# Attention over growing key blocks, masks added by TensorE, and weight splits moved between stages of a fused attention and expert kernel

## The reference

```python
q_sem, q_geo = 16 heads of 32; k_sem, k_geo, v = 4 groups;  q_geo, k_geo roped
remote = Tq - LW                      # 1024 - 128 = 896; nblk = 14 blocks of 64
pool = mean over each block of 64 for the first 896 keys, then the last 128 keys as they are
k_pos = concat(arange(14) * 64 + 63, arange(896, 1024))      # 142 keys
scores = (q_sem @ k_sem2 + q_geo @ k_geo2) / sqrt(32) * exp(logit_scale)
scores = where(k_pos <= pos, scores, -1e9)
out = softmax(scores) @ v2, then @ Wo
# expert branch: router softmax over 16 experts, top 4, weights normalised
out = sum over the 4 of weight * (silu(x @ gate) * (x @ up)) @ down
```

## Time and profile before

| What | Value |
|---|---|
| Median of 3 runs | 415.14 us |
| The profiled execution's own time | 414.26 us |
| Its span, first to last instruction | 412.5 us |
| TensorE busy | 367.9 us, 89% |
| VectorE busy | 263.2 us, 64% |
| ScalarE busy | 185.9 us, 45% |
| GpSimd busy | 233.3 us, 57% |
| Mean granted TensorE clock | 0.959 |

### The profile page before, as it was taken

How to read it: one execution, slowest core, us unless ns; L and a number is a source line. 1 busy time by engine, 2 the same in 40 slices (tenths; PEclk the granted TensorE clock), 3 DMA queues, 4 the chain that set the end, 5 groups by cost and what they waited for, 6 DMA issues and landing times.

```text
span 412.5 us, 8607 instructions
## 1 busy us (share of the span) xinstructions
PE 367.9 (89%) x2263; PEld 309.1 (75%) x2264; DVE 263.2 (64%) x837; ACT 185.9 (45%) x537; POOL 233.3 (57%) x205
## 2 busy tenths in 40 slices
PE   0599995968998999799899999999999999999991
PEld 0483474756885677577678899999999999999881
DVE  4889244897924799999857755555555555555540
ACT  1541236543521265225537655555555555555550
POOL 3501556566555435994605666566666666666664
PEclk9999997897999999999779999999999999999996
DMA  7991222212114963068545666676667667667544
GB/s 246 357 316 46 78 78 78 78 64 92 52 66 143 319 208 110 21 195 222 152 141 101 104 107 116 103 110 110 111 106 112 114 106 112 112 106 112 78 52 51
DMA packets 49016, 51.41 MB, mean 125 GB/s; under 512 B 5472, under 2 KB 46048, under 8 KB 48992
## 3 DMA queue, kind: packets, MB, share of 16 engines
q0 software_dynamic: 14640, 19.34, 28.3%
q1 hardware_dynamic: 34352, 31.78, 27.2%
HBM read 29.67 MB, written 21.43 MB: 124 GB/s over the span
## 4 chain that ended last, share of the span: by engine, by line
PE 71%; DVE 14%; issue 7%; ACT 3%; DMA 2%; SPq 1%; POOLq 1%; another core or an unknown queue 0%; DVEq 0%; ACTq 0%
PE bank L1292 59%; PE bank L1654 4%; PE bank L1678 4%; DMA x_all<-in_L_attn_x 1%; ACT lex L760 1%; DVE q L1073 1%; DVE q L1070 1%; ACT x_all L692 1%; PE bank L1445 1%; PE bank L1416 1%; DMA out_rows<-y,idx 1%; DVE l L1097 1%; DVE pr L1213 1%; DVE xr L1241 1%; DVE pr L1233 1%
## 5 line engine op out<-in xcount | busy, mean ns | idle before, releaser
L670 POOL DMA_INDIRECT out_rows<-y,idx x79 | 122.9, 1556 | 81.8 <-ACT y L854 63.2
L648 POOL DMA_INDIRECT xn_by_expert<-x_all,slot_i x64 | 64.9, 1014 | 20.4 <-issue 15.7
L1272 DVE SCALAR_TENSOR_TENSOR act<-bank,xg,sg 128x224 f32<-128x224 f32 x79 | 35.6, 450 | 51.5 <-ACT sg L841 50.7
L1292 PE MATMUL bank<-wgu_hi,xh 128*128 x158 | 65.2, 413 | 0.5 <-issue 0.2
L1292 PE MATMUL bank<-wgu_lo,xh 128*128 x158 | 58.5, 370 | 0.0
L1292 PE MATMUL bank<-wgu_hi,xl 128*128 x158 | 57.9, 366 | 0.0
L841 ACT ACTIVATE sg<-bank 128x224 f32<-128x224 f32 x79 | 28.3, 358 | 60.6 <-PE bank L1292 59.7
L1264 DVE TENSOR_TENSOR xl<-bank,xh 128x256 fp32r<-128x256 f32 x79 | 33.5, 424 | 29.4 <-ACT xh L834 29.1
L1292 PE MATMUL bank<-wdn_hi,ah 112*128 x158 | 51.3, 324 | 0.5 <-issue 0.4
L1292 PE MATMUL bank<-wdn_hi,al 112*128 x158 | 44.4, 281 | 0.0
L1292 PE MATMUL bank<-wdn_lo,ah 112*128 x158 | 44.2, 280 | 0.0
(11 more groups left out here) (238 smaller groups left out, 766.1 us busy)
## 6 DMA issues: line engine op xcount, KB each, us to landing
xg<-xn_by_expert SPq DMA_DIRECT2D x79, 129.0 KB, 2.5
wgu<-in_L_ffn_gate_proj SPq DMA_DIRECT2D x16, 224.0 KB, 5.4
wgu<-in_L_ffn_up_proj SPq DMA_DIRECT2D x16, 224.0 KB, 5.8
wdn<-in_L_ffn_down_proj SPq DMA_DIRECT2D x16, 224.0 KB, 6.2
x_all<-in_L_attn_x SPq DMA_DIRECT2D x8, 256.0 KB, 4.8
xr<-in_L_attn_x SPq DMA_DIRECT2D x14, 128.0 KB, 4.6
out_rows<-xr SPq DMA_DIRECT2D x14, 128.0 KB
out_rows<-y,idx POOLq DMA_INDIRECT x79
```

The source lines that it names most:

```text
L648: gp.indirect_dma_start(xs_d, bass.IndirectOffsetOnAxis(slot_i[:, z, r:r + 1], 0), x_all[:, z, :], None).then_inc(xs_in[q], DMA)
L670: gp.indirect_dma_start(out_rows, bass.IndirectOffsetOnAxis(idx[r % RING][:, 0:1], 0), ysb[r % 4][:, :], None, compute_op=ALU.add).then_in ...
L1272: nc.vector.scalar_tensor_tensor(av[t.par][:, :], bank[2 + t.par][:, I:2 * I], xg[t.slot][:, D + 1:D + 2], sg[t.par][:, :], ALU.mult, ALU. ...
L1292: return nc.tensor.matmul(o, lhsT, rhs, start=start, stop=stop)
```

## The change

Six things change together.

1. **Remote scores**: the columns are laid out block by block, with the 16 heads inside a block, so that tile t needs only the first 32(t+1) of 224 columns. Matmuls, exponentials and VectorE's operations take only those. For tiles 1 to 6 the mask is a bf16 matmul of the identity with `hide_b` over the last 32 columns, and VectorE reads maximum and subtraction directly from PSUM; the masking operation and the copy of `even` are gone. Tile 0 keeps the masking operation on 32 columns, and gets the even part through a matmul with the constant `even`. The probabilities need one transpose and one matmul for tiles 0 to 3 (plus the even part in tile 0), two after that.
2. **Local scores**: the mask is the first matmul into each bank (bf16, identity with `hide_lb`). VectorE takes four negated maxima directly from PSUM, one for each head, and ScalarE reads PSUM for the exponentials. The banks come free only when the exponentials are done, in two pairs of heads.
3. **Tables and folding**: `weights(2)`, `weights(3)`, the first part of the task plan and `bd_s` move ahead of the local queries on VectorE, the rest of the plan (`bound_tasks`) right behind them.
4. **Values**: `build_values` needs one multiplication per group, `sum_columns` goes. The folding with Wo is one matmul of 58 rows x 512 per group in units 3 to 6. Its rows go to DRAM and come back as `vw` in the new order: 12 writes and 3 reads on SyncE's queue.
5. **Splits**: ScalarE makes the high parts of experts 0 to 3 in remote pairs 0 and 1, 4 to 9 in pairs 3 to 5, 10 to 12 at the head of the expert loop, and 13 to 15 at steps 5, 6, 7. VectorE makes the low parts of 0 to 5 at the end of pairs 0 to 5 and 13 to 15 at steps 6, 7, 8. GpSimd makes 6 to 12, and starts when VectorE has made its six.
6. **SyncE**: the residual rows of pair 6 are loaded early, experts 10 to 12 in one group, 13 to 15 behind the first eight task loads.

```diff
-LATE = ((4, 5), (6, 7), (8, 9), (10, 11), (12,), (13, 14, 15))
+LATE = ((4, 5), (6, 7), (8, 9), (10, 11, 12), (13,), (14,), (15,))
-ON_DVE = 4
+ON_DVE = 6
-        SPLITS = ((), (4, 5), (6, 7), (8, 9), (), (10, 11), (12,))
+        SPLITS = ((0, 1), (2, 3), (), (4, 5), (6, 7), (8, 9), ())
+        HEAD = (10, 11, 12)
@@ ScalarE: local exponentials; head and steps of the loop
-                    last = nc.scalar.activation(lex[q][:, h, :], l2[q][:, h, :], ACT.Exp, bias=lneg[q][:, h:h + 1], accum_out=lsum[q][:, h:h + 1])
-                last.then_inc(l_ex, 1)
+                    nc.scalar.activation(lex[q][:, h, :], bank[L_BANKS[h]][:, 0:NKEY], ACT.Exp, bias=lneg[q][:, h:h + 1], accum_out=lsum[q][:, h:h + 1]).then_inc(l_ex, 1)
...
+                    for k in HEAD:
+                        split_late(k)
...
-                if j.counts is None and j.r in (1, 3, 5):
-                    split_late(IN_LOOP + j.r // 2)
+                if j.counts is None and j.r in (5, 6, 7):
+                    split_late(IN_LOOP + j.r - 5)
@@ SyncE: the folded values through DRAM
+            for g in range(HKV):
+                sp.wait_ge(fold_kept, g + 1)
+                for m in range(2):
+                    sp.dma_start(vw_rows[:, :, 2 * g + m, :], folded[g % 2][0:FOLD - NB, m, :]).then_inc(folded_out[g % 2], DMA)
...
+            sp.dma_start(vw[:, :, 0, :], by_batch[0:P, :, :]).then_inc(vw_in, DMA)
@@ VectorE: local scores
-                for h in range(G):
-                    last = nc.vector.tensor_tensor(l2[q][:, h, :], bank[L_BANKS[h]][:, 0:NKEY], hide_l, ALU.add)
-                last.then_inc(l_read, 1)
-                dve.wait_ge(l_read, n + 1)
-                link(nc.vector.tensor_reduce(lmax[q][:, :], l2[q][:, :, :], axis=AX.X, op=ALU.max))
-                nc.vector.tensor_scalar(lneg[q][:, :], lmax[q][:, :], -1.0, None, ALU.mult).then_inc(l_max, 1)
+                for h in range(G):
+                    last = nc.vector.tensor_reduce(lneg[q][:, h:h + 1], bank[L_BANKS[h]][:, 0:NKEY], axis=AX.X, op=ALU.max, negate=True)
+                last.then_inc(l_max, 1)
@@ VectorE: remote pairs
+                scores = bank[6 + u]
+                if t.first:
...
+                link(nc.vector.tensor_reduce(smax[u][:, :], by_head(scores, t), axis=AX.X, op=ALU.max))
...
+                nc.vector.tensor_tensor(by_key(pr[u], t), by_key(scores, t), over_heads(smax[u][:, :], t), ALU.subtract).then_inc(c_d[u], 1)
...
+                if t.number < ON_DVE:
+                    split_low(t.number)
@@ TensorE: local scores
-                    pe.wait_ge(l_read, n)
...
+                for two in ((0, 1), (2, 3)):
+
+                    if n:
+                        pe.wait_ge(l_ex, G * (n - 1) + two[1] + 1)
+                    for h in two:
+                        mm(bank[L_BANKS[h]][:, 0:NKEY], ident_b[:, :], hide_lb[:, :], True, False)
@@ TensorE: folding, remote scores
+                mm(bank[4][0:FOLD, :], vb[:, g, :], wo_s[:, 2 * g:2 * g + 2, :].rearrange("p m d -> p (m d)"), True, True).then_inc(fold_done, 1)
...
+                    mm(bank[6 + u][:, 0:t.cols], xT[t.number][:, u, c, :], asem[:, u, c, 0:t.cols], c == 0, False)
+                if not t.first:
+                    mm(bank[6 + u][:, t.cols - 2 * H:t.cols], ident_b[:, :], hide_b[:, :, :].rearrange("p k h -> p (k h)"), False, False)
```

337 lines of the change are left out of this document (174 added, 163 removed).

## The result

The changed kernel takes 419.43 us, the median of 20 executions (414.79 to 427.65), where the kernel before took 414.89 beside it (20 executions, 412.82 to 416.87). The ratio is 1.0083, 95% interval 1.0056 to 1.0110. Forecast was 398.5, a ratio near 0.96.

A forecast was written before the change was run, and what follows sets the result against it. Bounds: a TensorE-VectorE-ScalarE ring in the local units, VectorE in the remote pairs, TensorE in the expert loop. From 414.26 us profiled, -7.5 - 14.2 + 0 + 4.5 + 1 = -16.2 gave 398.1; stated 398.5, range 389.5 to 408.5.

The forecast's parts named there:

- Local units: Local attention stage: last exponentials end at 107.5, `l_attend` starts at 110.5 instead of 118.04 us, -7.5 us.
- The ring: Local units' cycle through TensorE, VectorE and ScalarE: 4.0 us a turn, 4.8 with value folding, 6.6 with queries too.
- Rival (d): Local units 2 to 7 and output products: TensorE idles each turn, clock stays at 1.2 GHz, 423 us; chance 0.08.
- Tables ahead and the values' way through DRAM: Before and during local units: tables hidden by VectorE's waits, DRAM trip ending near 113 us; 0 us each.
- Output products: Products between local units and remote pairs: stay at 13.0 us.
- Remote pairs: Remote attention: VectorE's pairs 0 to 5 take 53.5 us, first tokens turned at 185.6 instead of 207.35; -14.2 us.
- A page against it: VectorE's PSUM reads: a skill page's rule adds 65 ns to each of 60 operations, making 402.4 us.
- Head: Start of expert loop: ScalarE's three splits cost about 2.0 us, no lower clock gives -2.0; sum 0.
- GpSimd's gate: Expert loop: GpSimd's seven splits start after VectorE's sixth, so ScalarE's result 4 waits for the scatter; +4.5 us.
- T: End of VectorE's remote pair 5, forecast at 182.0 us; GpSimd's first result scatter lands at T + 29.9.
- Splits 13 to 15: Loop's head: these experts' splits in three consecutive steps instead of every second add VectorE work; +1 us.

The follow-up runs named there:

- e13_fill6: e10_early_fill5 plus a sixth fill, 6 throwaway TensorE products ahead of unit 7's scores: 404.09 us, ratio 0.9726.
- e11_before_fill: The kernel before plus 43 throwaway TensorE products at waits in local units 0, 1 and 4: 409.46 us, ratio 0.9913.
- e5_all_columns: The changed kernel with remote pairs 1 to 6 computing all 14 blocks' columns (output differs): 422.60 us, ratio 1.0177.
- e2_gate_after: The changed kernel with GpSimd's first subtraction waiting for VectorE's last product of probabilities and reciprocals: 419.48 us, ratio 1.0157.
- e9_early_fill3: The changed kernel with experts 13 to 15 loaded behind 10 to 12, their VectorE splits in steps 4, 6, 7, and three fills: 405.78 us, ratio 0.9816.
- e16_mid_fill6: e13_fill6 with its weight loads of experts 10 to 15 one pair sooner: 402.68 us, ratio 0.9709.
- e14_early_gate: e9_early_fill3 with GpSimd's first subtraction waiting for VectorE's last product of probabilities and reciprocals: 416.27 us, ratio 1.0025.
- e1_late_loads: The changed kernel with the nine loads of experts 13 to 15 issued directly behind those of 10 to 12: 412.26 us, ratio 0.9984.
- e17_mid_no_fill: The changed kernel with the loads of e16_mid_fill6, VectorE's splits of experts 13 to 15 in steps 4, 6, 7, and no fills: 411.82 us, ratio 0.9900.
- e10_early_fill5: e9_early_fill3 plus two fills, 16 throwaway products behind unit 0's scores and 20 in unit 2: 408.93 us, ratio 0.9775.
- e3_fill: The changed kernel plus 26 throwaway TensorE products at three idle places in the local units: 413.90 us, ratio 0.9949.

## Why the prediction was wrong, step by step

**Local units, -7.5 forecast, +3.5 measured: the step that failed.** The ring itself was sized about right. In e13_fill6 at the full clock, the exponentials of units 3 to 7 start 5.4, 5.0, 7.9 and 6.8 us apart, 25.0 in all, where 4.8, 4.8, 6.6 and 6.6 were summed, 22.8; 2.4 us of fills stand among them. What failed is what the sum took for granted: it let the lower clock follow only where it followed before, up to unit 3, and priced every term of the ring behind that from rows at the full clock. In the changed kernel TensorE was at the lower level for 20 of the 24 us from 100 to 124. With all fills, at a clock of 1.00, L is 48.2, 9.6 us shorter and near the 46.9 that the sum came to. Rival (d) named the mechanism, gave it 0.08, and put its price at 25 us; it came in part, not from unit 2 on and hardly in the output products. Its argument against, that TensorE is busy two thirds of each turn, was no protection. A second error stood in the baseline: the 54.4 us before held two low stretches (-6.5 us with fills, e11_before_fill), so most of the forecast gain could be had without this change.

**Tables ahead and the values' way through DRAM, 0 and 0: right** for what follows 65 us; the matmul that spreads the table costs TensorE 0.6 us ahead of the first score, and 1.0 of the 1.9 us was lost between 20 and 22.5 us, in transposes and products that took longer at the same clock of 1.00; why is open. The first local score lies between 64.1 and 66.1 us in the runs with this same opening, so part of the 1.9 is no work of the change. Output products: +0.6, at a clock of 0.96; 13.27 us at 1.00 in the other runs.

**Remote pairs, -14.2: right**, -13.0, and not by luck: VectorE's pairs 0 to 5 took 8.7, 8.8, 9.0, 8.8, 9.1 and 9.4 us, 53.8 in all where 53.5 was summed, and the first tokens were turned 4.6 us behind them, with a wait of 0.95 for the tile, where 3.6 was summed. Columns were worth 5.0 (e5_all_columns), and the stretched additions went, 693 ns each.

**A page against it.** Against the row: `smax<-bank` over 224 columns takes 386 ns,

```profile
L1242 DVE TENSOR_REDUCE smax<-bank 128x16 f32<-128x224 f32 x2 | 0.8, 386 | 0.5 <-PE bank L1322 0.5
```

and the same reduction from SBUF took 0.39 us. The 65 ns that the Trainium skill, "VectorE: DVE Perf Modes", section "The TRN2 errata — SBUF-src ops pay a fixed extra latency per instruction", would add for PSUM don't show here.

**Head, 0 forecast, +3.8: wrong.** I let the stretched operations disappear with GpSimd's work, and didn't see that its start, bound to VectorE's sixth split, falls on the last two products, which TensorE needs before the loop. e2_gate_after gives the price, 4.0 us. The forecast that the head would no longer run at the lower clock, -2.0, failed as well: it was at 0.50 from 203 to 210 us. The Trainium skill, "SBUF — State Buffer", section "Who interferes with whom", says that an instruction of VectorE with two SBUF inputs contends with one of GpSimd that reads SBUF, over a shared port pair that is an exclusive lock. The trace agrees: the two products took 2.57 and 2.26 us and ended at 203.17 and 205.35, each some 0.25 us behind the end of a subtraction of GpSimd (202.91 and 205.10).

**GpSimd's gate, +4.5: right in its date by luck, wrong in its price.** T + 29.9 was to bring the fifth result to ScalarE; T is 196.27, and it came at 226.49, T + 30.2:

```profile
226.49 0.37 ACT L897 COPY y<-bank 128x256 f32<-128x256 f32 x1 [2.18 <-DMA out_rows<-y,idx]
```

Two errors cancel in it: from GpSimd's start to its first scatter 26.5 us were summed and 23.9 were taken, from there to the result 3.39 were summed and 6.3 were taken. But the head ran 3.8 us late, which used up most of this stall, and the token tile came as late as the result. With early loads E is within 0.8 us of before (e9_early_fill3, e16_mid_fill6): the gate's own price there is at most that. It has no slack left: a start that waits for the last products costs 4.6 us of E (e14_early_gate).

**Splits 13 to 15, +1: mis-sized**, a wait of 2.5 (E falls by 2.3 from e1_late_loads to e17_mid_no_fill), and by another way: not VectorE's load but the place of the last split ahead of task 10's wait.

**SyncE's late loads were not a term at all.** The text followed the edit's place and not its queue: nine loads ahead of the ninth token tile cost 3.5 us (e1_late_loads).

## What to carry to other kernels

Before you sum a stage, mark where its clock is low and what TensorE did ahead of it: part of the stage's time is that, and here a change that kept the gaps and added waits on a third engine widened it. Throwaway matmuls in the gaps, behind the same semaphores (68 of 0.12 us here), test this in one run and may stay in the kernel. Count the low stretches of the baseline as well: fills alone gave the kernel before 0.9%. When a transfer or another engine's start is moved, ask what it then stands ahead of, in its queue and on the port it shares; here the same nine loads cost 3.5 us too late, 3.4 us too early, and nothing one pair sooner.

## What the runs showed of the hardware that was not expected

- Gaps of 0.9 and 1.0 us stood ahead of 20 us mostly at the lower clock, and one of 0.46 us ahead of 14 (e10_early_fill5); in e3_fill and e9_early_fill3 the same 0.46 us had no fall behind it, nor had one of 1.62 us in e11_before_fill and one of 1.05 in e16_mid_fill6. So a gap's length alone doesn't decide it; what does is open.
- bf16 products of 256 columns at 0.12 us each kept the clock up, in this kernel and in the one before.
- GpSimd beside VectorE cost VectorE 4.0 us on two products, and about 9 us of busy time over three pairs.
- One execution of the changed kernel took 1725 us, once in 143 executions of it and its variants; it isn't explained.
